# AdaLN attention and mixture of experts on one core: prologue by halves of the tokens, inverse roots begun on Pool, side work moved to other units

## What is computed

```python
B, T, D = 2, 1024, 128; H, HD = 16, 8
mod = (silu(c) @ wmod).reshape(B, 6, 1, D)
sa, ca, ga, sb, cb, gb = (mod[:, k] for k in range(6))
ga = (2 * (ga >= 0) - 1) * maximum(abs(ga), 0.25)     # gb likewise
h = layernorm(x) * (1 + ca) + sa
# scores = h h^T / sqrt(8) per head, times 1 where two tokens have the same index modulo 8, else times sigmoid(w)
x = x + ga * (softmax(scores * mask) @ h)
h = layernorm(x) * (1 + cb) + sb
top_p, top_i = top_k(softmax(h @ router_W + router_b), 3)
x = x + gb * (relu(h @ sW1 + sb1) @ sW2 + sb2 + sum_e cw_e * (relu(h @ eW1[e] + eb1[e]) @ eW2[e] + eb2[e]))
```

## Time and profile before

| | us |
|---|---|
| median of 3 runs | 406.41 (405.30 to 407.01) |
| the profiled execution | 404.34 |
| its span, first to last instruction | 402.5 |
| PE busy | 353.2 (88%) |
| ACT busy | 291.0 (72%) |
| DVE busy | 243.3 (60%) |
| POOL busy | 29.1 (7%) |
| first and last exponential start | 27.6 and 292.5 |

### The profile page before, as it was taken

One profiled execution on the slowest core, in us unless ns is written; L12 is line 12 of the kernel. 1 busy time (PEld: TensorE's weight loads), 2 busy tenths in 40 slices (PEclk: granted clock), 3 DMA queues, 4 the chain that ended last, 5 costly groups with the idle time before them and its releaser, 6 DMA issues.

```text
span 402.5 us, 6490 instructions
## 1 busy us (share of the span) xinstructions
PE 353.2 (88%) x2435; PEld 164.9 (41%) x2435; DVE 243.3 (60%) x627; ACT 291.0 (72%) x270; POOL 29.1 (7%) x55
## 2 busy tenths in 40 slices
PE   1768897898999989698698999988998999999995
PEld 1663233232332323233232222322355757777773
DVE  5868473843543669493724444423068999778784
ACT  2646997889999889497849999989943344444442
POOL 3166000004000113000000000000000000000000
PEclk9997999989999999899969999999999999999999
DMA  5000200030000000000002100006620029833000
GB/s 166 1 4 1 90 24 2 3 106 2 2 1 2 5 4 3 4 2 2 2 4 65 45 0 2 1 2 234 266 104 2 0 67 413 333 107 104 26 2 26
DMA packets 9626, 22.40 MB, mean 56 GB/s; under 512 B 1452, under 2 KB 5964, under 8 KB 8056
## 3 DMA queue, kind: packets, MB, share of 16 engines
q1 hardware_dynamic: 9176, 21.95, 15.3%
q10 hardware_dynamic: 416, 0.00, 0.1%
HBM read 20.55 MB, written 1.17 MB: 54 GB/s over the span
## 4 chain that ended last, share of the span: by engine, by line
PE 52%; DVE 22%; ACT 11%; issue 10%; DMA 2%; SPq 1%; DVEq 0%; ACTq 0%
PE acc L1158 17%; ACT prob L556 10%; PE slot L1059 9%; PE spare L1010 5%; DVE KK L735 4%; PE slot L1187 3%; PE slot L1188 3%; PE slot L1189 3%; PE slot L1212 3%; PE slot L1209 2%; PE slot L1210 2%; PE slot L1204 2%; DVE QQ L735 2%; DVE oT L835 2%; DVE bH L762 2%
## 5 line engine op out<-in xcount | busy, mean ns | idle before, releaser
L556 ACT ACTIVATE prob<-slot 128x1536 f32<-128x1536 f32 x171 | 235.6, 1462 | 35.8 <-PE slot L1059 35.2
L1158 PE MATMUL acc<-prob,val 128*9 128x512 f32 x1024 | 138.0, 612 | 13.1 <-DVE oT L835 12.1
L1059 PE MATMUL slot<-QQ,KK 32*128 32x512 f32 (+1 forms) x768 | 91.2, 410 | 12.3 <-ACT prob L556 7.6
L1059 PEld LDWEIGHTS slot<-QQ,KK 32*128 32x128 f32 x768 | 44.1, 188 | 114.9 <-ACT prob L556 77.4
L585 ACT ACTIVATE ghi<-prob 128x512 fp32r<-128x512 f32 x52 | 32.9, 632 | 50.1 <-DVE prob L962 50.1
L835 DVE COPY oT<-acc 128x512 f32<-128x512 f32 x16 | 11.0, 690 | 47.9 <-PE acc L1158 47.9
L970 DVE SCALAR_TENSOR_TENSOR glo<-prob,ghi 128x512 fp32r<-128x512 f32 x52 | 35.6, 684 | 0.4
L1158 PEld LDWEIGHTS acc<-prob,val 128*9 128x9 f32 x1024 | 15.6, 88 | 42.9 <-issue 37.0
L962 DVE SCALAR_TENSOR_TENSOR prob<-slot,bcol,KK 128x512 f32<-128x512 f32 x37 | 27.6, 750 | 6.8 <-PE slot L1189 6.4
L1187 PE MATMUL slot<-h2hi,w1h 128*128 128x512 f32 x64 | 30.6, 478 | 0.0
L841 DVE RECIPROCAL rden<-spare 128x16 f32<-128x16 f32 x16 | 4.1, 258 | 40.8 <-PE spare L1010 40.8
(11 more groups left out here) (178 smaller groups left out, 315.6 us busy)
## 6 DMA issues: line engine op xcount, KB each, us to landing
KK<-cw_d SPq DMA_DIRECT2D x7, 1024.0 KB, 9.9
rows<-cw_d SPq DMA_DIRECT2D x5, 1024.0 KB, 5.2
KK<-cw_d SPq DMA_DIRECT2D x3, 768.0 KB, 9.6
rows<-in_L_ffn_eW SPq DMA_DIRECT2D x2, 960.0 KB, 5.3
xz<-in_L_attn_x SPq DMA_DIRECT2D x2, 512.0 KB, 5.3
att<-in_L_attn_x SPq DMA_DIRECT2D x4, 256.0 KB, 3.4
out<-att SPq DMA_DIRECT2D x4, 256.0 KB, 3.5
QQ<-shrow SPq DMA_DIRECT2D x56, 4.0 KB
```

Source lines behind the costliest of these rows:

```text
L556: nc.scalar.activation(ring[:, at:at + n * CH], slot[u % 2][:, 0:n * CH], ACT.Exp, scale=SCALE).then_inc(exp_done, 1)
L1059: return mm(dst, KK[n][r, s, c * M:(c + 1) * M], QQ[n][r, lo:hi], start=True, stop=True, tile_position=(32 * q, 0))
L1158: last = mm(acc[32 * q:32 * q + HD + 1], val[:, b, n, c, q, :], prob[:, (G * cl + q) % RING], start=c == 0, stop=c == C - 1, tile_position ...
```

## The change

1. x of batch 0 comes in two halves, c as two rows, `wmod` in two halves on ScalarE's queue. Moments, roots, rows and transposes of the first half alone stand before the attention; the second half of group 0 becomes a side build at unit 2. ScalarE instead of Pool spreads the columns of group 0; Pool spreads the others, does the gate and `vrow`, and normalises the value rows that ScalarE normalised. The twelve products with ones go.
2. An inverse root is Pool's power (exponent -0.5) and one Newton step on DVE: DVE writes the variance, waits for Pool, and does three instructions.
3. The table of side work is a list: builds of batch 1 at the units 67 and 70, 78 and 81, 89 and 92, 100 and 103, in order before the turn of the same unit; "bias" at 41; the second norm, router and weights of stages 0 to 2 at new units; the splits of the weights at 153, 155, 157 and 163, 165, 167; the router's last three pieces one unit apart.

```diff
+BUILDS = ((0, 0, (None, 2)), (0, 1, (5, 8)), (0, 2, (15, 18)), (0, 3, (25, 28)), (1, 0, (67, 70)), (1, 1, (78, 81)),
+          (1, 2, (89, 92)), (1, 3, (100, 103)))
+BIAS_UNIT = 41
+SECOND_UNIT = 36
+ROUTE = ((47, 51, 53, 58, 63), (111, 115, 117, 122, 127), (132, 136, 138, 142, 148))
+SPLIT_W2, SPLIT_W1 = 153, 163
...
-    for n, units in ((1, (1, 4)), (2, (15, 18)), (3, (26, 29))):
...
-        told += [(e + 9, ("h2T", p, 0, 0)), (e + 14, ("logit", p, 0, 0)), (e + 24, ("cwT", p, 0, 0))]
-    for n, units in ((0, (end_unit(5) + 4, end_unit(5) + 7)), (1, (end_unit(6) + 3, end_unit(6) + 5)),
-                     (2, (end_unit(6) + 8, end_unit(7) + 7)), (3, (end_unit(8) + 7, end_unit(9) + 4))):
...
-                sp.dma_start(xz[:, 0], x[0].rearrange("(m c) d -> m c d", c=C)).then_inc(ld_x[0], 16)
-                sp.dma_start(wm, wmod).then_inc(ld_wm, 16)
+                for half in range(HALVES):
+                    sp.dma_start(xz[:, 0, QC * half:QC * half + QC], tokens(x, half)).then_inc(ld_x[half], 16)
...
+            def root_guess(lo, hi):
+                asked[0] += 1
+                pool.wait_ge(var_ok, asked[0])
+                p.tensor_tensor(rstd[:, 1, lo:hi], rstd[:, 0, lo:hi], power[:, 0:hi - lo], ALU.pow
+                                ).then_inc(guess_ok, 1)
+
+            root_guess(0, QC)
+            pool.wait_ge(ld_wm[0], 16)
+            for k in range(2):
+                for n in range(1, NG):
+                    spread_weights(p.tensor_copy, k, n).then_inc(wmr_ok, 1)
+            pool.wait_ge(mod_ok, 4)
+            p.tensor_scalar(ga_abs, ga_abs, 0.25, None, ALU.max).then_inc(pool_seq, 1)
...
+            for half in range(HALVES):
+                if half:
+                    root_guess(QC, C)
+                pool.wait_ge(root_ok, half + 1)
...
+            act.dma_start(crow[:, 0], cvec).then_inc(ld_c, 16)
...
+                act.dma_start(wm[:, 0:3 * D], wmod[:, 0:3 * D]).then_inc(ld_wm[0], 16)
+                act.dma_start(wcol[:, 0:1], ipw.partition_broadcast(128)).then_inc(ld_ipw, 16)
+                act.dma_start(wm[:, 3 * D:6 * D], wmod[:, 3 * D:6 * D]).then_inc(ld_wm[1], 16)
...
+            for k in range(2):
+                spread_weights(nc.scalar.copy, k, 0).then_inc(first_wmr, 1)
...
+            def inverse_root(lo, hi, chain):
+
+                var, y, t = (rstd[:, j, lo:hi] for j in range(3))
+                v.tensor_scalar(var, mv[:, lo:hi, 1], EPS, None, ALU.add).then_inc(var_ok, 1)
+                asked[0] += 1
+                dve.wait_ge(guess_ok, asked[0])
+                chain(v.tensor_tensor(t, y, y, ALU.mult))
+                chain(v.scalar_tensor_tensor(t, t, -0.5, var, ALU.mult, ALU.mult))
+                return v.scalar_tensor_tensor(y, t, 1.5, y, ALU.add, ALU.mult)
...
+            first_rows(0)
...
+            dve.wait_ge(first_ok, 3)
+            operand(KK[0][:, 0], half_cols(0), ffT[:], m_key, oT[:]).then_inc(built[0], 1)
+
+            first_rows(1)
...
-            def keep_busy(times):
-                for _ in range(times):
-                    mm(slot[0][:, CH:CH + 128], ones[:], ones[:], start=True, stop=True)
...
+            other_columns().then_inc(side_mm, 1)
             exact = exact_wanted(pe)
...
-            side(("bias", 0, 0, 0))
             pe.wait_ge(built[0], 1)
             pe.wait_ge(acc_ok, 1)
             for u in range(UNITS):
-                if u == 1:
-                    pe.wait_ge(first_ok, 6)
                 scores(u)
```

More of the change, by code:

```diff
@@ new lines, in _ @@
+            for half in range(HALVES):
+                if half:
+                    root_guess(QC, C)
+                pool.wait_ge(root_ok, half + 1)
+                pool.wait_ge(ld_x[half], 16)
+                for c in range(QC * half, QC * half + QC):
+                    last = p.tensor_scalar(z[0][:, c], xz[:, 0, c], mv[:, c, 0:1], rstd[:, 1, c:c + 1], ALU.subtract,
+                                           ALU.mult)
+                last.then_inc(z_ok, 1)
+            pool.wait_ge(z_ok, HALVES)
```

357 lines of the change are left out of this document (176 added, 181 removed).

## The result

The changed kernel takes **394.73 us** (median of four runs, 393.12 to 396.5), the kernel before 405.86 us in the same comparison (403.06 to 407.01): a ratio of **0.9729**, 95% interval 0.9683 to 0.9775. The profiled execution took 396.5 us, the longest of its four, with a span of 394.7 us; the one of before took 404.34.

What follows compares the result with a forecast made beforehand. It took ACT's exponentials and TensorE as nearly co-critical, ACT's idle time all waiting for TensorE's scores. Gains 6 + 10.4 + 0.6 = 17.0 from 404.34 gave 387.3, plus 2.07 to the median: 389.4 us, range 381.5 to 399.

Steps and rivals of the forecast that it cites:

- the likeliest case: Whole kernel: the forecast itself, 389.4 us, own range 385 to 394, chance 0.54.
- Start, up to unit 0: Prologue to the first exponential: with half the loads and classes first, it starts at 17.4 instead of 27.63, 10.2 us earlier.
- Start, up to unit 5: First unit with keys of group 0's second half: starts about 30.4 instead of 38.31, 7.9 us earlier.
- The forecast's own sign of being wrong: At the start: unit 5 later than 33 would mean Pool's power or the load of `wmod` above its bound.
- Start, up to unit 10: Second group's first unit: starts at 39.4 instead of 45.1, gain 6 us, bounds 2 and 9.
- four units at the low level: Around unit 5, after TensorE idles some 5 us: four units at 1.2 GHz, taking 1.88 instead of 1.36, cost 2 us.
- Sections' ends: Waits at the attention's section ends: 18.6 us saved less 8.2 added, net 10.4 us, bounds 0 and 17.
- The pairs: A build and a turn in one unit, at 25, 67, 78 and 89: TensorE waits for the bank, 6.7 us cost.
- Experts: Expert stretch at the end: eight root instructions fall away, one Pool wait comes; gain 0.6 us, between 0 and 1.6.
- The products with ones at nothing: Before the first scores: dropping these TensorE products costs nothing, as they bought 3.4 us at full clock at most.
- the start is eaten: Rival at the start: low clock over the first ten units, second build 2 us later; 394.4 us, chance 0.12.
- ends give nothing: Rival at the sections' ends: pairs cost as much as late copies, or PE is the bound; 399.8 us, chance 0.13.

Runs made afterwards that it cites:

- rows on ACT: Changed kernel with Pool's eight value rows of batch 0 normalised on ACT instead: 391.95 us, ratio 0.9671 to the kernel before.
- early build: Changed kernel with the first half of group 1's build at unit 4 instead of 5: 394.34 us, ratio 0.9703 to the kernel before.
- order alone: Kernel before with only the new table of side work, its old prologue and roots kept: 393.47 us, ratio 0.9722 to the kernel before.
- The experiment's ones: Changed kernel with seven products of ones put back before the first scores, behind TensorE's jump: 393.8 us, ratio 0.9732 to the kernel before.
- start alone: Changed kernel with all side work at its old places, so new start and roots only: 403.62 us, ratio 0.9968 to the kernel before.

## Why the prediction was right, and where its steps were not

The range (381.5 to 399) held the time, and the sign was right; the number was 5.3 us too low, and the time lies just outside the range of the likeliest case (385 to 394). The measured gain of 11 us is made up otherwise than forecast: in the profiles -1.4 us up to unit 10, -3.8 from there to unit 18, 12.1 from there to the last exponential and 0.9 in the experts, 7.8 together and not 11, since the profiled execution of the changed kernel was its longest. That the range held owes to its width and to a good forecast for the sections' ends; the start's mechanism was wrong by 7 us.

- **Start, up to unit 0:** 10.2 us forecast, 7.5 came. TensorE's jump was read off as the 1.1 us idle behind the ones and priced at that; the branch took 3.62 us then, mostly under the ones, and takes 3.85 now with little over it. From the columns' end (15.2, forecast 15.6) to the scores it was 3.99 us instead of 1.1, which makes up the loss. A shorter jump alone would not have helped: DVE's last operand was ready only at 18.58, where the forecast had 15.3. Some 1.5 us of that is a later begin (11.75, not 10.2), and the rest slow instructions beside Pool: 3.9 us (14.69 to 18.58) for a cast and three products, two of which took 1.09 and 1.21 instead of 0.75.
- **Start, up to unit 5:** forecast 30.4, came 35.0. DVE asked for the power at 19.98, 3.3 us later than in the forecast (15.3 and 1.4 for the moments), for the reason above. Pool's four rows, "1.1 us", took 4.06 and held the power until 21.39, another 1.4; it had been 17.5. The power took 1.04, not 0.5, and so was above its bound. So of the 4.6 us roughly 2.5 are DVE's lateness, 1.4 the rows on Pool beyond it, and half a microsecond each the power and the side build. The rows on ACT gave back 1.9, which fits. DVE's jump (3.82 for 4.06) was right. The side build took 5.5 us for 5. The forecast's own sign of being wrong, unit 5 later than 33, came.
- **Start, up to unit 10:** "Gain 6 us" was the step that fell; it became a loss of 1.4, outside its bounds of 2 and 9. Besides the 4.6 us from unit 5, the transposes of group 1's build stand behind unit 5's scores and product on TensorE, so DVE idled 3.77 us, where the forecast left 1.4 between two builds. The early build confirmed the place and showed the next link. The last term, 3.6 us from the build's end to the scores, was right (42.29 to 45.91).
- **Behind unit 10:** four units at the low level had been priced at 2 us before unit 10; a second spell after it, which the forecast does not have, cost 3.8 in the profiled execution.
- **Sections' ends:** 10.4 forecast; the order alone gave 0.9722, 11.3 us, and 12.4 in its profile. The pairs were put at 6.7 us and show 7.1 in ACT's timeline; that they came from the bank was right, but only half could be had back by parting them. The part of the forecast that the gain rests on was right in its mechanism and near in its size.
- **Experts:** 0.6 forecast, 0.9 came, within its bounds.
- **The products with ones at nothing:** not tested, and probably not quite nothing. The experiment's ones stood behind the jump and didn't raise the level, so it shows only that such ones don't help. The row for granted clock reads 1.00 from 20 to 30 us in the changed kernel, and yet a class's products took 1.90 us there, as at 0.50 in the kernel with ones; so TensorE was at the low level there, and the column shows it only from the first change on. The Trainium skill, "TensorE: Matmul & The Clock Gate", section "Part 1: The HAM clock gate", says the throttled clock is the default; by that rule the trace agrees. What the level costs here can be read from start alone, which is the same program up to unit 10: its granted clock was 1.00 from 32.3 to 35.7, unit 5's class took 1.05 us instead of 1.89, and unit 10 came 0.8 us earlier (45.7 against 46.5). Ahead of that TensorE waits for DVE's rows, Pool's values and DVE's keys (1.83, 1.82 and 1.43 us), so a higher level had little to give up to unit 5; that is argued, not shown.
- **The rivals:** the second, "the start is eaten", gave 394.4 by a low level over ten units and a second build 2 us late. Its number was the nearest, but by luck: the low level was there in units 0 to 5 and again after 10, not over the first ten, and the second build ended at 42.3, 6.5 us later than forecast, not 2. Pool's rows (2.0 us by their experiment), TensorE's jump at its full length and the order of its queue (1.5 at unit 10) were in no case, nor that DVE works slower beside Pool, whose share was not taken apart. The first (ends give nothing) is refuted by the order alone.

## What to carry to other kernels

A head start at the first unit counts only if the chain to the unit that waits next is shorter too: write out that chain (here DVE, Pool, TensorE's in-order queue, four small loads) before you price the start. Price an instruction on another engine by a row of that very form on that engine, and where none exists keep the bound far out; and keep two uses of one bank out of the same unit, which gave back about half of their price here. An idle time behind a jump is only what the work ahead of the jump leaves uncovered: look up the branch itself before you carry that number over. When one wait is cut, look at once at what is issued last in each queue, since that is the next wait.
